# Masked attention behind a layer norm: each block of scores issued in two halves, one per unit, and the turned outputs moved forward

## What is computed

```python
h = jnp.maximum(_layernorm(x, axis=-1), 0.0)
q = (h @ Wq + bq).reshape(b, n, H, HD)      # k and v alike
scores = jnp.einsum('bihd,bjhd->bhij', q, k) / jnp.sqrt(jnp.float32(HD))
mask = jnp.where(adj == 0, jnp.float32(-1000000000.0), jnp.float32(0.0))
weights = jax.nn.softmax(scores + mask[None, None, :, :], axis=-1)
out = jnp.einsum('bhij,bjhd->bihd', weights, v)
x = x + out.reshape(b, n, H * HD)
```

## Time and profile before

| | |
|---|---|
| time, median of 3 runs | 4070.03 us (4066.47 to 4071.05) |
| the profiled execution's own time | 4066.34 us |
| its span, first to last instruction | 4064.5 us |
| first transposes of unit 0, block 0 | 64.73 us from the span's start |
| PE busy | 4017.7 us (99%) |
| DVE busy | 3064.8 us (75%) |
| ACT busy | 3077.6 us (76%) |

### The profile page before, as it was taken

How to read it: one execution, slowest core, us unless ns; L and a number is a source line. 1 busy time by engine, 2 the same in 40 slices (tenths; PEclk the granted TensorE clock), 3 DMA queues, 4 the chain that set the end, 5 groups by cost and what they waited for, 6 DMA issues and landing times. The chain is left out here.

```text
span 4064.5 us, 64393 instructions
## 1 busy us (share of the span) xinstructions
PE 4017.7 (99%) x22016; PEld 3277.6 (81%) x22016; DVE 3064.8 (75%) x5128; ACT 3077.6 (76%) x5514; POOL 1401.6 (34%) x1409
## 2 busy tenths in 40 slices
PE   7999999999999999999999999999999999999998
PEld 6888888888888888888888888888888888888886
DVE  6877867777777777777777687776877868768686
ACT  5877868778687786877868688686886868868687
POOL 4333333333333333333333333333333333333322
PEclk9999999999999999999999999999999999999999
DMA  5232223222223232222222232222322313223121
GB/s 183 69 93 63 85 59 84 86 65 83 70 72 86 66 85 80 62 83 80 74 81 64 78 92 61 81 79 64 93 66 77 85 59 91 83 59 98 38 73 47
DMA packets 239955, 314.83 MB, mean 77 GB/s; under 512 B 16401, under 2 KB 147473, under 8 KB 231057
## 3 DMA queue, kind: packets, MB, share of 16 engines
q1 hardware_dynamic: 239632, 310.71, 26.8%
HBM read 172.23 MB, written 37.75 MB: 52 GB/s over the span
## 5 line engine op out<-in xcount | busy, mean ns | idle before, releaser
L830 DVE TENSOR_TENSOR pT<-T,pT 128x512 fp32r<-128x512 f32 x2048 | 1390.7, 688 | 750.2 <-ACT pT L665 733.4
L665 ACT CAST pT<-T 128x512 fp32r<-128x512 f32 x2048 | 1186.1, 591 | 656.4 <-PE T L546 575.4
L824 DVE CUSTOM_DVE_ANT_0 S<-S,mask 128x1024 f32<-128x1024 f32 x1024 | 1252.1, 1223 | 3.1 <-PE S L535 3.1
L546 PE MATMUL T<-ident,probs 128*128 128x128 f32 x8192 | 1231.8, 273 | 1.0 <-ACT probs L673 0.6
L546 PEld LDWEIGHTS T<-ident,probs 128*128 128x128 f32 x8192 | 1006.6, 140 | 277.7 <-DVE pT L830 41.4
L673 ACT ACTIVATE probs<-S,negmax 128x1024 f32<-128x1024 f32 x1024 | 1151.5, 1124 | 8.4 <-DVE negmax L824 5.2
L565 PE MATMUL O<-pT,vs 128*64 128x512 f32 x2048 | 964.5, 471 | 0.2 <-DVE pT L830 0.2
L558 PE MATMUL O<-pT,vs 128*128 128x512 f32 x2048 | 816.1, 398 | 0.0
L504 PE MATMUL misc<-hT,wqk 128*128 128x512 f32 x3036 | 787.4, 395 | 7.7 <-ACT y L656 7.7
L504 PEld LDWEIGHTS misc<-hT,wqk 128*128 128x128 f32 x3036 | 556.9, 188 | 160.7 <-issue 42.9
L409 POOL TENSOR_TENSOR outs<-outs,oT 64x512 f32<-64x512 f32 x256 | 336.1, 1313 | 562.4 <-DMA outs<-oT 556.2
(11 more groups left out here) (70 smaller groups left out, 3587.5 us busy)
## 6 DMA issues: line engine op xcount, KB each, us to landing
wqk<-wqk_split SPq DMA_DIRECT2D x63, 1024.0 KB, 7.1
xln<-in_x SPq DMA_DIRECT2D x240, 256.0 KB, 2.7
outs<-in_x SPq DMA_DIRECT2D x66, 512.0 KB, 4.8
kA<-kA SPq DMA_DIRECT2D x128, 256.0 KB, 3.2
kB<-kB SPq DMA_DIRECT2D x128, 256.0 KB, 3.8
outs<-oT SPq DMA_DIRECT2D x256, 128.0 KB, 3.1
out<-outs SPq DMA_DIRECT2D x64, 512.0 KB, 4.4
probs<-in_adj SPq DMA_DIRECT2D x4, 1024.0 KB, 5.0
```

The source lines that it names most:

```text
L546: mm = pe.transpose(T[:, u % 2, i * P:(i + 1) * P], probs[:, (GB * g + i) % RING, j * P:(j + 1) * P], ident[:])
L665: act.copy(pT[:, u % PT, 0, :], T[:, u % 2, :]).then_inc(p_hi, 1)
L824: dve.tensor_tensor_reduce(S[:, s % 2, :], S[:, s % 2, :], mask[:, s % NB, :], 1.0, 3.0e38, ALU.add, ALU.min, negmax[:, s % RING:s % RING ...
L830: dve.tensor_tensor(pT[:, u % PT, 1, :], T[:, u % 2, :], pT[:, u % PT, 0, :].bitcast(F32), ALU.subtract).then_inc(p_lo, 1)
```

## The change

Three things change. `score_ahead` issues one half of a score block (512 keys, two matmuls) in the even unit and the other half in the odd unit behind it; the waits stay with the first half and the `scored` signal with the second, so that DVE's `shift` moves from the even unit to the odd one (`due`). ACT's `exponential` of a block stays in the same even unit. `turn_out` on PE moves from behind `contract_hi` to directly behind `turn_probs`, and `copy_y` on ACT from behind the exponential to in front of it. On SP, the load of an x tile (units of `HT_AT`) is issued ahead of `copy_k` of the same unit, and the second `copy_k` comes one unit later.

```diff
-COPY_K_AT, STORE_AT, RES_AT, WQK_AT = (8, 15), 19, 24, (21, 21, 28, 21)
+COPY_K_AT, STORE_AT, RES_AT, WQK_AT = (8, 16), 19, 24, (21, 21, 28, 21)
+HALVED = tuple(range(0, UNITS, 2))
...
-            def score(b, s):
+            def score(b, s, halves=(0, 1)):
...
+                if 0 in halves:
+                    pe.wait_ge(q_low, 4 * pair + 3 + (s // 8) % 2)
+                    pe.wait_ge(k_copied, 64 * (pair + 1))
+                    if some(n - 1):
+                        pe.wait_ge(exped, n - 1)
+                for half in halves:
...
-                mm.then_inc(scored, 1)
+                if 1 in halves:
+                    mm.then_inc(scored, 1)
...
-                if u % 2 == 0 and s < SBLOCKS:
-                    score(b, s)
+                halves = (u % 2,) if u // 2 * 2 in HALVED else (0, 1) if u % 2 == 0 else ()
+                if halves and s < SBLOCKS:
+                    score(b, s, halves)
...
                         turn_probs(b, u)
-                        score_ahead(b, u, last)
-                        contract_hi(b, u - LAG)
                         if u in OUT_AT and not first:
                             turn_out(b - 1, PAIRS - 1, OUT_AT.index(u), before(b, u, True, last))
                         if u >= PER and u % PER in OUT_AT:
                             turn_out(b, u // PER - 1, OUT_AT.index(u % PER), before(b, u, True, last))
+                        score_ahead(b, u, last)
+                        contract_hi(b, u - LAG)
...
                     probs_hi(b, u)
+                    if u in OUT_AT and not first:
+                        copy_y(b - 1, PAIRS - 1, OUT_AT.index(u))
...
                     probs_low(b, u)
                     s = u // 2 + LEAD
-                    if u % 2 == 0 and s < SBLOCKS:
+                    due = u % 2 == (1 if u // 2 * 2 in HALVED else 0)
+                    if due and s < SBLOCKS:
                         shift(b, s)
```

More of the change, by code:

```diff
@@ L323, in body @@
                         load_xln(b + 1, (t + XLN) % NB)
-                    for half in range(2):
-                        if v == COPY_K_AT[half] and not (last and p == PAIRS - 1):
-                            copy_k(b, p + 1, half)
                     if u in HT_AT and HT_AT[u] + XLN < NB and not last:
@@ L330, in body @@
                         load_xln(b + 1, t + XLN)
+                    for half in range(2):
+                        if v == COPY_K_AT[half] and not (last and p == PAIRS - 1):
+                            copy_k(b, p + 1, half)
                     if v == WQK_AT[p] and not (last and p >= PAIRS - 2):
@@ L578, in score_ahead @@
                 s = u // 2 + LEAD
-                if u % 2 == 0 and s < SBLOCKS:
-                    score(b, s)
-                if u % 2 == 0 and s >= SBLOCKS and not last:
-                    score(b + 1, s - SBLOCKS)
+                halves = (u % 2,) if u // 2 * 2 in HALVED else (0, 1) if u % 2 == 0 else ()
+                if halves and s < SBLOCKS:
+                    score(b, s, halves)
+                if halves and s >= SBLOCKS and not last:
+                    score(b + 1, s - SBLOCKS, halves)
             def fill(b, u, last):
@@ L751, in body @@
                     probs_hi(b, u)
+                    if u in OUT_AT and not first:
+                        copy_y(b - 1, PAIRS - 1, OUT_AT.index(u))
+                    if u >= PER and u % PER in OUT_AT:
+                        copy_y(b, u // PER - 1, OUT_AT.index(u % PER))
                     s = u // 2 + LEAD - 1
@@ L756, in body @@
                         exponential(b + 1, s - SBLOCKS)
[L757 to L760, removed]
                     if u in V_SPLIT_AT and not (last and u > V_FROM):
@@ L890, in body @@
                     s = u // 2 + LEAD
-                    if u % 2 == 0 and s < SBLOCKS:
+                    due = u % 2 == (1 if u // 2 * 2 in HALVED else 0)
+                    if due and s < SBLOCKS:
                         shift(b, s)
-                    if u % 2 == 0 and s >= SBLOCKS and not last:
+                    if due and s >= SBLOCKS and not last:
                         shift(b + 1, s - SBLOCKS)
```

## The result

| | before | after |
|---|---|---|
| median | 4069.31 us (4066.47 to 4071.05, 4 runs) | 4665.8 us (4665.04 to 4667.82, 4 runs) |
| ratio | | 1.1467, 95% interval 1.1453 to 1.1482 |
| span of the profiled execution | 4064.5 us | 4664.4 us |

What follows compares the result with a forecast made beforehand. PE was taken to set the pace, then to follow a 3.65 us cycle: 34.5 - 2.7 + 2.4 = +34.2 us in 15 blocks (513) plus 42 in the last, on 4066.3, gives 4621, stated as 4620; range 4510 to 4730.

Steps and rivals of the forecast that it cites:

- What bounds the kernel: PE sets the pace at 2.73 us for two units without fills; its small waits are worth about 65 us.
- The cycle: Units without fills: exponential, cast, low part, shift, next exponential stand in line, 3.65 us for two units against PE's 2.73.
- The stretches: Per pair of heads, last fill to next pair's first: losses 10.5 us twice, 8.3, 5.2; +34.5 us per block.
- F + 41.3: Transposes at v = 35, counted from F, when PE goes on after the v = 12 fill; before, F + 30.77.
- Waits that go: PE's waits at v = 3, v = 5 and before v fills at odd units vanish: -2.7 us per block.
- The wait that comes: Early outputs wait for misc's evacuation at four v = 10 and unit 2: 0.49 us each, +2.4 us per block.
- The sum: 34.5 - 2.7 + 2.4 = +34.2 us in each of 15 blocks, 42 in the last: 4621 us.
- The clock rival: PE's regular idling of about 0.9 us in every 3.65 halves its clock: some 5580 us; 6%.
- The fills pay nothing back: Rival: lateness from units without fills stays through the units with fills, 4711 us; 9%.
- The strict order of ACT and DVE: Both queues are first-in, first-out, so no cast passes a waiting exponential; this gives the 3.65 us.
- the faster rival: Only PE's small waits change, gaining about 65 us less up to 38: 4005 to 4030 us; 5%.

Runs made afterwards that it cites:

- chosen places: Changed kernel halved at only eight even units, outputs and y early only at v = 2 of pairs 1 to 3: 4027.1 us, ratio 0.9896.

## Why the prediction was right

- **What bounds the kernel**: right. Without the small waits (chosen places) the gain is 42 to 47 us, of some 65 that PE's timeline held.
- **The cycle, 3.65 us for two units**: right, 3.70 measured. The error is mainly in one link: from the read of the minimum to the exponential I took 0.17 us (0.14 and 0.03), and it is 0.24; from the cast to the low part it is 0.60 and not 0.62. With a copy of O it turns in 4.18 to 4.19, so the copy adds 0.49 and not 0.60.
- **The stretches**: F + 41.3 against 41.44; the third 43.0 against 43.8; the fourth 21.8 against 22.2. In sum 35.8 us per block (means of 13 blocks) where the prediction had 34.5. The two errors of the cycle, +0.05 in ten turns and -0.11 in three, nearly cancel. What is too much in the third stretch is not the cycle's: its ten turns take 40.8 us, as foreseen (39.04 and three casts at 0.58), but the transposes behind unit 98 stand only 0.4 us ahead of the exponential and not 1.2. These 0.8 us per block come from the outputs' wait at unit 98, a wait that the prediction put at nothing.
- **Waits that go**: 2.7 us per block foreseen, about 2.05 found: 3 x 0.36 at v = 3, 0.65 before the v fills, and at v = 5 2 x 0.21 at units 5 and 101, but 2 x -0.06 at units 37 and 69, where the fill still waits 0.20 us and more. There the step that failed is that all four vanish: the exponential of unit 36 is late from the cycle and stands in front of the evacuation. That starts 0.70 us behind PE's next work, not 0.20:

```profile
2452.03 0.39 PE L561 MATMUL O<-pT,vs 128*128 128x512 f32 x1
...
2452.73 0.68 ACT L692 ACTIVATE proj<-misc,bqk 128x512 f32<-128x512 f32 x1
```

- **The wait that comes**: right places but for unit 98, and a wrong size. 0.49 us foreseen, about 0.7 at the four v = 10 and 0.6 at unit 2, 3.4 us per block and not 2.4. This is the term of the sum that was mis-sized most, in relation. The step that failed is "PE reaches the wait ... at 0.43 us, 0.20 + 0.69 + 0.03": at v = 10 ACT starts its evacuation 0.29 us behind PE's transposes (2397.57 against 2397.28), where the step had it 0.20 behind the start of PE's next work, and the outputs start 0.15 us behind its end, where the step had 0.03.
- **The sum**: +34.2 us per block foreseen, 37.1 found (from unit 0 of block 0 to unit 0 of block 15, 4325.2 against 3768.9 us); the terms above give 35.8 - 2.05 + 3.4 = 37.15. The last block lost 45 us, 42 foreseen. In all 4620 against 4665.8, inside the range. All terms of the sum came out dearer than foreseen, so nothing cancels between them.
- **The clock rival** is out as a price: PE idled in nearly every turn, and the granted clock of a whole pair's stretch is 1.00, as the view of windows shows (busy us of PE, PEld, DVE, ACT and POOL, then the clock):

```profile
2404.00:2447.00 43.00, 37.30 (x191) 25.14 (x190) 28.25 (x51) 28.14 (x51) 11.28 (x13) 1.00 0.29 83
```

  But the clock did fall once between the start-up and the end, to its level of 1.2 GHz, right behind the wait at unit 98 of block 1 (PE's timeline and the windows):

```profile
562.28 0.94 PE L577 MATMUL misc<-ident,outs 128*128 128x128 f32 x4 [1.40 <-DVE hT L801]
...
562.50:565.80 3.30, 3.30 (x13) 2.60 (x12) 2.34 (x4) 2.15 (x4) 1.79 (x2) 0.50 0.17 40
```

  It was back at the full level some 3.4 us later, and the block took 289.9 us where its neighbour took 288.3: 1.6 us. At the other 14 waits of 1.40 us it did not fall. The Trainium skill's rule that short idle times make the clock go up and down ("TensorE: Matmul & The Clock Gate", "A second HAM failure mode: psum-queue depth-cycling") thus showed itself once here and not in the turns, where PE loses 0.97 us in every 3.70.
- **The fills pay nothing back**: nearly all is paid back. Of the late exponentials only the 0.27 us at units 37 and 69 reach PE; beside them and the wait at v = 10 it lost nothing from v = 3 to v = 13.
- **The strict order of ACT and DVE**, the Trainium skill's rule in "TensorE: Matmul & The Clock Gate", Part 1: the trace agrees. In the turn above the transposes that start at 2419.84 have ended by 2420.50, and ACT stands idle until 2421.08; yet their cast does not pass the waiting exponential and starts behind it, at 2422.18. And moving one call by a line on DVE changed the time by 321 us.
- **Slips in the working**: the faster rival's upper end is 4005 + 38 = 4043 and not 4030; a turn of the sum is 39.04 / 10 = 3.90 us in the mean, where the clock rival was priced with 3.75; and if the copies of O hid, that would be worth 10 x 16 x 0.60 = 96 us and not 40. None of them enters the forecast.

## What to carry to other kernels

Before moving an operation nearer to its consumer, write down the cycle through the engines' orders: follow the moved operation to its consumer, then to what stands behind that in the consumer's queue, and on until you are back. If the sum is longer than the pace of the engine that sets the time, that engine will follow the cycle, however idle the others are. Work that fills a wait for a buffer belongs only where that wait is found: the same halves cost 573 us everywhere, and at eight places, with the outputs early only at v = 2 of three pairs of heads, the kernel gained 42 to 47 us. Where such work is moved, look also at what the late engine does for others: the outputs at unit 98 waited for an evacuation that stood behind a late exponential.

## What was not expected of the hardware

The step from DVE's minimum to ACT's exponential took 0.24 us from the start of the read where the exponential waited for it (2420.84 to 2421.08; the median of all 1024 is the same), of which the read is 0.14; the step from ACT's cast to DVE's low part left 0.03. Which part of the remaining 0.10 is the semaphore and which the exponential's own start is open. It was not tried. Nor is it known why the clock fell behind one wait of 1.40 us and not behind 14 others, nor in the run with the exponential one unit later, where PE waited up to 1.67 us again and again.
